# Combination weights turned in one product, output bias as high and low rows: two small TensorE steps of a two-layer hybrid block

## The chip, the cores and the metric

The kernel runs on one core of a Trainium2 chip. The metric is the time of one launch on the device in microseconds (us), the median of several runs. The core has TensorE (PE, matrix products; its weight loads are listed as PEld), VectorE (DVE), ScalarE (ACT), GpSimd (POOL), and SyncE (SP), which here only issues DMAs. Products land in eight banks of PSUM, `bank[0]` to `bank[7]`; PE, DVE and ACT can reach them, POOL works in SBUF.

## The reference

Four rows of 1024 tokens with 128 features in fp32 pass four residual steps. Cut to what matters here:

```python
x = x + attn_a(layernorm(x))     # per-token linear attention over 16 heads, then an MLP
x = x + ffn(layernorm(x))        # 32 experts, top 8
x = x + attn_b(layernorm(x))     # causal window of 64 keys, 16 heads of 8
x = x + ffn(layernorm(x))        # the same experts again

# ffn
probs = softmax(x @ gate_w.T)                 # 32 experts
top_w, top_idx = top_k(probs, 8); top_w /= sum(top_w)
comb = sum(one_hot(top_idx, 32) * top_w)      # a weight per token and expert, most are 0
out = sum_e comb[:, e] * ((x @ up_e.T) * silu(x @ gate_e.T)) @ down_e.T

# the end of attn_b
return ctx @ w_out.T + b_out
```

All 32 experts are computed for all tokens; `comb` weighs their hidden units.

## The kernel before, in words

Work goes in groups of 512 tokens (`GT`), four blocks of 128 (`T = 4`). A row has two groups. There are 16 expert stages (4 rows, 2 groups, 2 ffn steps). A stage is 16 chunks of 128 hidden units (two experts of 64). For a chunk `n`, PE makes the gate and the up product, each as three f32r products of high and low parts (L1522 to L1524); ACT applies silu (L1064); DVE multiplies with the up product (L1303); POOL multiplies with the combination weights `spread_w` (L881, the "hidden units"); and PE adds the down product to bank 6 (`down`, L1545), which in fp32 is two passes. `down` runs three chunks behind (`LAG`), and ACT, DVE and POOL each have a queue of their own, in order.

All other steps (norms, routing, linear attention, projections) are put between the chunks by a table, `PLAN`, that names for each stage or attention part and each slot the steps to run there. Every engine runs its part of a step at that slot. The attention parts (`"attn"`) have slots of their own, three per tile of 128 tokens. The PE steps share bank 7, `side`: a step waits until the reader of the step before has raised `side_taken` (`side_free`), and its reader waits for `side_ready`.

The steps that the change touches:

- `weighT`, 16 times: after `cnorm` (ACT, L1026) has normed `comb`, [128 tokens, 4 blocks, 32 experts], PE turns it (L1460), four transposes into `side[0:32]`; ACT copies that to `combT` (L1033), 32 partitions of 512 tokens, and then frees `side`. SP's `send_weights` (L664) stores `combT` to `comb_dram`, waits for the landing, and issues the loads that spread each expert's weights over 64 partitions (L676, L681). These feed POOL's hidden units of the next stage.
- `proj`, 8 times: the output projection of attn_b. PE first puts the bias into `side` for all four blocks: one row of ones times one row of bias, in fp32 (L1493). Then four fp32 products with `out_w` add to it (L1497). It stands at slot 20 of the first attention part (group 0), in slot 26 of the later ones, and for group 1 at slot 3 of the next row's first expert stage (of the last rows at like places).
- `mask_rest`, once, on POOL (L814 on): the last of the constants.

The chain of `proj` at slot 3 (`(1, "first")`) begins when `pick` on POOL (L895, L897) has finished `mixT`.

Of the kernel before, what the change touches and what calls it, by code (L numbers as in the profile page):

```python
# [19 lines left out]
F32 = mybir.dt.float32  # L20
F32R = mybir.dt.float32r
BF16 = mybir.dt.bfloat16
I32 = mybir.dt.int32
ALU = mybir.AluOpType
ACT = mybir.ActivationFunctionType
AX_X = mybir.AxisListType.X

P = 128
ROWS, SEQ, D = 4, 1024, 128
T = 4  # L30
GT = T * P
# [4 lines left out]
NE, ED = 32, 64  # L36
# [5 lines left out]
QB = 32  # L42
# [13 lines left out]
DEEP = 3  # L56
# [399 lines left out]
def hybrid_block(nc, x, wqkv_a, lam, g1, g2, g3, w1, w2, wqkv_b, wout, bout, wgate, wg, wu, wd, out):  # L456
# [3 lines left out]
    with ExitStack() as ctx:  # L460
        def sb(name, shape, dt=F32):
            return ctx.enter_context(nc.sbuf_tensor(name, shape, dt))

        def sem(name):
            return ctx.enter_context(nc.semaphore(name))
# [2 lines left out]
        qkv_a_w = sb("qkv_a_w", [P, 3 * D])  # L468
        w1_w, w2_w = sb("w1_w", [P, D]), sb("w2_w", [P, D])
        qkv_b_w, out_w = sb("qkv_b_w", [P, 3 * D]), sb("out_w", [P, D])  # L470
        bout_row = sb("bout_row", [1, D])
        router_w = sb("router_w", [P, NE])
        gate_hi, gate_lo = sb("gate_hi", [P, NE * ED], F32R), sb("gate_lo", [P, NE * ED], F32R)
        up_hi, up_lo = sb("up_hi", [P, NE * ED], F32R), sb("up_lo", [P, NE * ED], F32R)
# [4 lines left out]
        lam_diff, lam_coef = sb("lam_diff", [P, 1]), sb("lam_coef", [P, 1])  # L479

        ident, same_query = sb("ident", [P, P]), sb("same_query", [P, HG, QB], BF16)
        ones_row, ones_col, minus_half = sb("ones_row", [1, P]), sb("ones_col", [P, 1]), sb("minus_half", [P, 1])
        head_bits, head_mask = sb("head_bits", [P, HG, HG]), sb("head_mask", [P, HG])
        q_mask = sb("q_mask", [P, HG])
        window = sb("window", [P, 2, NB, KW], BF16)
# [22 lines left out]
        logits, top, neg_top = sb("logits", [P, T, NE]), sb("top", [P, T, TOP]), sb("neg_top", [P, T])  # L508
        expd, replaced = sb("expd", [P, T, NE]), sb("replaced", [P, T, NE])
        top_sum, top_inv = sb("top_sum", [P, T]), sb("top_inv", [P, T])  # L510
        comb, combT = sb("comb", [P, T, NE]), sb("combT", [NE, 2, GT])

        comb_dram = nc.dram_tensor("comb_dram", (DEEP, NE, GT), F32, kind="Internal").ap()
        spread_w = sb("spread_w", [P, 2, EACH, GT])
# [16 lines left out]
        side = bank[SIDE_BANK]  # L531

        x_loaded, x_stored = [[sem(f"x_loaded_{r}_{g}") for g in range(G)] for r in range(2)], (sem("x_stored_0"), sem("x_stored_1"))
        qkv_a_loaded, attn_a_loaded, small_loaded, down_loaded = (
            sem("qkv_a_loaded"), sem("attn_a_loaded"), sem("small_loaded"), sem("down_loaded"))
        gate_loaded, up_loaded = sem("gate_loaded"), sem("up_loaded")
        pool_const, ident_ready, masks_ready = sem("pool_const"), sem("ident_ready"), sem("masks_ready")
        lam_step, qkv_w_ready, bits_ready, head_mask_ready = (
            sem("lam_step"), sem("qkv_w_ready"), sem("bits_ready"), sem("head_mask_ready"))
        hi_ready, router_ready = sem("hi_ready"), sem("router_ready")  # L540
# [3 lines left out]
        side_ready, side_taken = sem("side_ready"), sem("side_taken")  # L544
# [16 lines left out]
        comb_ready, comb_normed, combT_ready, combT_sent = (  # L561
            sem("comb_ready"), sem("comb_normed"), sem("combT_ready"), sem("combT_sent"))
# [15 lines left out]
        qkv_a_loads = [(qkv_a_w[:], wqkv_a), (g1_col[:], g1.rearrange("(p a) -> p a", a=1))]  # L578
        attn_a_loads = [(lam_row[:], lam.partition_broadcast(P)), (g2_row[:], g2.partition_broadcast(P)),
                        (g3_row[:], g3.partition_broadcast(P)), (w1_w[:], w1), (w2_w[:], w2), (router_w[:], wgate)]  # L580
        small_loads = [(qkv_b_w[:], wqkv_b), (out_w[:], wout), (bout_row[:], bout.rearrange("(a n) -> a n", a=1))]

        def wait(engine, semaphore, count):

            if count > 0:
                engine.wait_ge(semaphore, count)
# [7 lines left out]
        def tile(row, i):  # L594
            return row * TILES + i
# [46 lines left out]
        def _(sp):  # L642
# [17 lines left out]
            def send_weights(fg):  # L660
                sp.wait_ge(combT_ready, fg + 1)
                for of_parity, loaded in enumerate(spread_loaded):
                    wait(sp, loaded, 32 * (1 + of_parity) * (fg - 2))
                sp.dma_start(comb_dram[fg % DEEP], combT[:, fg % 2]).then_inc(combT_sent, 16)  # L664
                sp.wait_ge(combT_sent, 16 * (fg + 1))

            def spread_quarter(fg, q):
# [30 lines left out]

            load_rows(1, 0)
            send_weights(0)  # L700
            spread_quarter(0, 0)
            spread_quarter(0, 1)
# [5 lines left out]
            def next_weights(fg):  # L708
                send_weights(fg)
                spread_quarter(fg, 0)  # L710
                spread_quarter(fg, 1)
# [14 lines left out]
            for period, place, row, f in SCHEDULE:  # L726
# [11 lines left out]
                fg = STAGE_AT[row, f]  # L738
# [18 lines left out]
        def _(pool):  # L757
            consts, steps_done = [0], [0]

            def const(ins):  # L760
                consts[0] += 1
                ins.then_inc(pool_const, 1)
                pool.wait_ge(pool_const, consts[0])
# [8 lines left out]
                               pattern=[[-1, P]], channel_multiplier=1).then_inc(ident_ready, 1)  # L772
            const(pool.memset(ones_col[:], 1.0))
            const(pool.memset(minus_half[:], -0.5))
            const(pool.memset(ones_row[:], 1.0))

            def w_lo(row, n):
                if n == 0:
# [8 lines left out]
            def masks(row, n):  # L787
                (mask_identity, mask_first, mask_rest)[n]()
# [13 lines left out]
            def mask_rows(groups):  # L802
                for j in groups:
                    rows = window[QB * j:QB * (j + 1)]
                    const(pool.affine_select(out=rows, in_=rows, compare_op=ALU.is_gt, fill=NEG, base=0,
                                             pattern=[[0, 2], [0, NB], [1, KW]], channel_multiplier=-1))
                    const(pool.affine_select(out=rows, in_=rows, compare_op=ALU.is_ge, fill=NEG, base=WIN,
                                             pattern=[[0, 2], [0, NB], [-1, KW]], channel_multiplier=1))
# [5 lines left out]
            def mask_rest():  # L814
                pool.wait_ge(kv_terms_ready, TILES)
                mask_rows(range(1, HG))
                for b in range(WIN // QB):
                    const(pool.memset(window[:, 0, b, 0:WIN - QB * b], NEG))

                const(pool.memset(vals[0:WIN, 0, 0], 0.0))  # L820
                pool.memset(keysT[:, 0:WIN], 0.0).then_inc(masks_ready, 1)

# [98 lines left out]
        def _(act):  # L921
# [4 lines left out]
            def side_product(row, name, n):  # L926
                act.wait_ge(side_ready, SIDE_AT[row, name, n] + 1)
# [101 lines left out]
            def weighT(row, f):  # L1029
                fg = STAGE_AT[row, f]  # L1030
                side_product(row, "weighT", f)
                wait(act, combT_sent, 16 * (fg - 1))
                act.activation(combT[:, fg % 2], side[0:NE, :], ACT.Copy).then_inc(combT_ready, 1)  # L1033
                act.wait_ge(combT_ready, fg + 1)
                act.sem_inc(side_taken, 1)

# [29 lines left out]
            def here(name, copy):  # L1066
# [5 lines left out]
                     "qscale": qscale, "h_sq1": h_sq1, "h_sq2": h_sq2, "h_gain": h_gain, "attnT": attnT_step,  # L1072
                     "mlp1": mlp1, "z_hi": z_hi_step, "weigh": weigh, "cnorm": cnorm,
                     "weighT": weighT, "seq_turn": here("seq_turn", seq_turn), "keys": here("keys", keys),
                     "queries": here("queries", queries), "values": values, "seq_copy": seq_turn, "keys_copy": keys,
                     "queries_copy": queries, "lam": lam_step_exp, "lead": lambda row, n: silu(row, 0, n)}
# [314 lines left out]
        def _(pe):  # L1391
            def side_free(row, name, n):
                wait(pe, side_taken, SIDE_AT[row, name, n])
# [62 lines left out]
            def weighT(row, f):  # L1456
                pe.wait_ge(comb_normed, STAGE_AT[row, f] + 1)
                side_free(row, "weighT", f)
                for t in range(T):
                    mm = pe.transpose(side[0:NE, P * t:P * (t + 1)], comb[:, t], ident[:])  # L1460
                mm.then_inc(side_ready, 1)

            def y_back(row, f):
                pe.wait_ge(y_copied, STAGE_AT[row, f] + 1)
# [23 lines left out]
                mm.then_inc(side_ready, 1)  # L1488

            def proj(row, g):  # L1490
                side_free(row, "proj", g)
                pe.wait_ge(mix_picked, tile(row, T * g + T))
                pe.matmul(side.rearrange("p (t d) -> p t d", d=D), ones_row[:],  # L1493
                          bout_row[:].unsqueeze(1).broadcast_to([1, T, D]), start=True, stop=False,
                          skip_group_check=True)
                for t in range(T):
                    mm = pe.matmul(side[:, P * t:P * (t + 1)], mixT[:, T * g + t], out_w[:], start=False,  # L1497
                                   stop=(t == T - 1), skip_group_check=True)
                mm.then_inc(side_ready, 1)

            def gate_up(row, f, s):
# [10 lines left out]
                for w_hi, w_lo, banks, freed, ready in ((gate_hi, gate_lo, GATE_BANKS, silu_ready, gate_ready),  # L1512
# [5 lines left out]
                    elif after is not None:  # L1518
# [8 lines left out]
                     "moe_turn": lambda row, n: turn(row, "m", n, "moe_turn"),  # L1527
                     "seq_turn": lambda row, n: turn(row, "s", n, "seq_turn"), "qkv": qkv_step, "qkv_first": qkv_first, "qkv_next": qkv_next, "attnT": attnT_step,
                     "mlp1": mlp1, "mlp2": mlp2, "route": route, "weighT": weighT, "y_back": y_back, "keys": keys,
                     "queries": queries, "values": values, "proj": proj,  # L1530
                     "early": lambda row, n: gate_up(row, 0, n)}

# [147 lines left out]
```

## Time and profile before

| what | value |
|---|---|
| three runs | 998.98, 1000.45, 1000.55 us (median 1000.45) |
| span of the profiled execution | 997.6 us, from its first to its last instruction |
| around the span | the runs lie 1.4 to 3.0 us above it; the profiled execution's own time is not listed apart |
| busy | PE 91%, POOL 66%, DVE 65%, PEld 63%, ACT 61% |

The profile has a page of sums and a trace of every instruction. Times in rows are us from the span's start unless they say ns. "x4" means four like instructions merged into one row, and the time is then that of all of them. In square brackets stands the idle time of the engine before the instruction and what ended it; "issue" means that nothing the profile shows was waited for. An fp32 product appears as two passes (x2). In rows of the chain a product's time is the part of it that the chain passes through; in the timeline its end is modelled and overlaps the next one.

### The profile page before, as it was taken

The numbers are of one execution on the slowest core, as the hardware profiler recorded it, in microseconds if no ns is written. First come the engines' busy times: TensorE is split into PE (matmuls) and PEld (weight loads), VectorE is DVE, ScalarE is ACT, GpSimd is POOL, SyncE is SP. The second block draws the span as 40 slices with busy tenths as digits, with TensorE's granted clock in tenths as the row PEclk, the third lists the DMA queues.
The fourth block names the chain that finished last, engine by engine and source line by source line (L and its number), as shares of the span: only waits on it lengthen the run. The fifth ranks groups of instructions, "written<-read, shape, count | busy, mean of one in ns | idle before, by whom it ended". The sixth has DMA issues, their size and how long they took to land.

```text
span 997.6 us, 16805 instructions
## 1 busy us (share of the span) xinstructions
PE 911.7 (91%) x5472; PEld 627.0 (63%) x5472; DVE 647.7 (65%) x1447; ACT 611.6 (61%) x1875; POOL 661.2 (66%) x610
## 2 busy tenths in 40 slices
PE   3267899899999999999999999999999998999998
PEld 1144566686666666586666666677666666657665
DVE  5886867688658638697739737787735347437432
ACT  4345566984664575895674575797455377386432
POOL 7676878657688649666759857756765545646554
PEclk8567999989999999999999999999999999999999
DMA  5005252014353524610433534520333560350452
GB/s 185 0 3 135 46 129 72 16 45 108 88 127 87 121 79 96 155 44 12 96 87 88 127 98 85 146 65 18 84 99 81 139 156 12 84 132 12 85 129 63
DMA packets 64762, 85.68 MB, mean 86 GB/s; under 512 B 5218, under 2 KB 30627, under 8 KB 64419
## 3 DMA queue, kind: packets, MB, share of 16 engines
q1 hardware_dynamic: 64674, 84.62, 35.2%
q8 instruction: 43, 0.70, 0.3%
q14 instruction: 45, 0.36, 0.1%
HBM read 79.32 MB, written 5.28 MB: 85 GB/s over the span
## 4 chain that ended last, share of the span: by engine, by line
PE 61%; ACT 11%; POOL 7%; issue 5%; DVE 4%; DVEq 0%; ACTq 0%; POOLq 0%
PE bank L1545 16%; PE bank L1522 8%; PE bank L1524 8%; PE bank L1523 8%; ACT probs L1089 5%; PE bank L1581 4%; PE bank L1566 4%; POOL work L881 3%; PE bank L1595 2%; PE bank L1559 1%; PE bank L1405 1%; POOL kv_terms L846 1%; DVE probsT L1345 1%; PE bank L1399 1%; POOL rstd L833 1%
## 5 line engine op out<-in xcount | busy, mean ns | idle before, releaser
L881 POOL TENSOR_TENSOR work<-work,spread_w 128x512 f32<-128x512 f32 x256 | 336.3, 1325 | 165.4 <-DVE work L1303 162.3
L1303 DVE TENSOR_TENSOR work<-work,bank 128x512 f32<-128x512 f32 x256 | 173.6, 681 | 214.0 <-ACT work L1064 128.1
L1545 PE MATMUL bank<-work,down_w 128*128 128x512 f32 x512 | 263.9, 599 | 9.3 <-POOL work L881 7.4
L1064 ACT ACTIVATE work<-bank 128x512 f32<-128x512 f32 x256 | 151.2, 596 | 182.1 <-PE bank L1524 178.6
L1089 ACT ACTIVATE probs<-bank,neg_max 128x96 f32<-128x96 f32 x512 | 166.0, 382 | 8.2 <-DVE neg_max L1331 5.7
L1522 PE MATMUL bank<-z_hi,gate_hi 128*128 128x512 f32 x256 | 167.0, 652 | 3.6 <-ACT elu L974 2.0
L889 POOL TENSOR_TENSOR probs<-probs,prob_inv 128x768 f32<-128x768 f32 x64 | 94.1, 1470 | 74.0 <-DVE prob_inv L1339 74.0
L1089 ACT ACTIVATION_READ_ACCUMULATOR probs<-bank,neg_max 128x1 f32 x512 | 125.6, 248 | 0.0
L1545 PEld LDWEIGHTS bank<-work,down_w 128*128 128x128 f32 x512 | 94.6, 189 | 40.5 <-POOL work L881 15.0
L1524 PE MATMUL bank<-z_hi,gate_lo 128*128 128x512 f32 x256 | 102.4, 400 | 0.0
L1522 PE MATMUL bank<-z_hi,up_hi 128*128 128x512 f32 x256 | 102.0, 398 | 0.0
L1523 PE MATMUL bank<-z_lo,gate_hi 128*128 128x512 f32 x256 | 101.6, 397 | 0.0
L1524 PE MATMUL bank<-z_hi,up_lo 128*128 128x512 f32 x256 | 101.5, 397 | 0.0
L1523 PE MATMUL bank<-z_lo,up_hi 128*128 128x512 f32 x256 | 100.5, 393 | 0.0
L846 POOL TENSOR_TENSOR kv_terms<-elu,qkv 128x1024 f32<-128x1024 f32 x32 | 84.7, 2649 | 12.7 <-DVE elu L1161 9.8
L1345 DVE COPY probsT<-bank 96x512 f32<-96x512 f32 x128 | 80.4, 667 | 7.1 <-PE bank L1581 6.5
L1331 DVE TENSOR_REDUCE neg_max<-bank 128x4 f32<-128x384 f32 x128 | 64.9, 547 | 23.4 <-PE bank L1566 22.4
L1581 PE MATMUL bank<-ident,probs 128*96 128x128 f32 x512 | 70.9, 281 | 8.2 <-DVE probsT L1345 7.0
L1522 PEld LDWEIGHTS bank<-z_hi,gate_hi 128*128 128x128 f32 x256 | 49.1, 192 | 40.0 <-issue 28.0
L1566 PE MATMUL bank<-keysT,qm 32*128 32x96 f32 x1024 | 70.0, 272 | 0.0
L1523 PEld LDWEIGHTS bank<-z_lo,gate_hi 128*128 128x128 f32 x256 | 49.5, 193 | 32.7 <-issue 29.8
L1566 PEld LDWEIGHTS bank<-keysT,qm 32*128 32x128 f32 x1024 | 67.4, 191 | 0.0
(154 smaller groups left out, 1466.2 us busy)
## 6 DMA issues: line engine op xcount, KB each, us to landing
spread_w<-comb_dram SPq DMA_DIRECT2D x96, 512.0 KB, 6.7
spread_w<-comb_dram SPq DMA_DIRECT2D x128, 128.0 KB, 3.0
vals<-v_dram SPq DMA_DIRECT2D x16, 384.0 KB, 4.1
x_buf<-x SPq DMA_DIRECT2D x8, 256.0 KB, 3.4
v_dram<-v_tok SPq DMA_DIRECT2D x8, 256.0 KB, 4.5
out<-xs SPq DMA_DIRECT2D x8, 256.0 KB, 3.8
spread_w<-wg SPq DMA_DIRECT2D x1, 1024.0 KB, 6.5
spread_w<-wu SPq DMA_DIRECT2D x1, 1024.0 KB, 8.5
```

Of the source, the lines that this page charges most:

```text
L846: pool.tensor_tensor(kv_terms[:, i % 2].rearrange("p (e d h) -> p e d h", e=HD, d=HD), k.unsqueeze(2).broadcast_to([P, HD, HD, H]), v.unsq ...
L881: pool.tensor_tensor(work[:, n % WORK], work[:, n % WORK], spread_w[:, n // EACH % 2, s % EACH], ALU.mult).then_inc(hid_gated, 1)
L889: pool.tensor_tensor(pr, pr, prob_inv[:, i % 2, part].unsqueeze(2).broadcast_to([P, HALF_BLOCKS, KW]), ALU.mult).then_inc(probs_normed, 1)
L1064: act.activation(work[:, n % WORK], bank[GATE_BANKS[ring_of(row, f, s)]], ACT.Silu).then_inc(silu_ready, 1)
L1089: a = act.activation(probs[:, i % 2, m], bank[hg][:, b * KW:(b + 1) * KW], ACT.Exp, bias=neg_max[:, i % 2, m:m + 1], accum_out=prob_sum[:, ...
L1303: dve.tensor_tensor(work[:, n % WORK], work[:, n % WORK], bank[UP_BANKS[ring_of(row, f, s)]], ALU.mult).then_inc(gated_ready, 1)
L1522: pe.matmul(dst, w_hi[:, cols], h, start=True, stop=False)
L1523: pe.matmul(dst, w_hi[:, cols], l, start=False, stop=False)
L1524: pe.matmul(dst, w_lo[:, cols], h, start=False, stop=True).then_inc(ready, 1)
L1545: pe.matmul(bank[Y_BANK], down_w[:, c], work[:, n % WORK], start=(c == 0), stop=(c == CH - 1)).then_inc(down_done, 1)
L1566: mm = pe.matmul(bank[hg][:, KW * b:KW * (b + 1)], qm[feats, i // T, NB * (i % T) + b].rearrange("p j q -> p (j q)"), keysT[feats, first:f ...
L1581: mm = pe.transpose(bank[4 + b % 2][0:KW, P * hg:P * (hg + 1)], probs[:, i % 2, hg * NB + b], ident[:])
```

## The change

The four transposes of a turn become one: `comb` is read as [128 tokens, 128 (block, expert)], and its transpose has (block, expert) in partitions. `combT` becomes 128 partitions of 128 tokens, and the store to `comb_dram` puts each partition's 512 bytes at its block's place; the layout there, and all that reads it, is as before. The bias becomes a matrix of 128 rows that is zero but for row 0, the bias rounded to f32r, and row 32 (`QB`), what the rounding left over; a 128x128 matrix of ones times it, in f32r, gives the bias for all four blocks in one product of one pass. POOL makes both matrices in `mask_rest`, and SP loads the bias a second time, into row 32.

```diff
-        bout_row = sb("bout_row", [1, D])
+        bout_rows = sb("bout_rows", [QB + 1, D])
+        bias_hi, bias_parts = sb("bias_hi", [QB + 1, D], F32R), sb("bias_parts", [P, D], F32R)
...
-        comb, combT = sb("comb", [P, T, NE]), sb("combT", [NE, 2, GT])
+        comb, combT = sb("comb", [P, T, NE]), sb("combT", [T * NE, 2, P])
...
+        small_loads = [(qkv_b_w[:], wqkv_b), (out_w[:], wout), (bout_rows[0:1], bout.rearrange("(a n) -> a n", a=1)),
+                       (bout_rows[QB:QB + 1], bout.rearrange("(a n) -> a n", a=1))]
...
-                sp.dma_start(comb_dram[fg % DEEP], combT[:, fg % 2]).then_inc(combT_sent, 16)
+                sp.dma_start(comb_dram[fg % DEEP].rearrange("e (t p) -> t e p", p=P),
+                             combT[:, fg % 2]).then_inc(combT_sent, 16)
...
-            const(pool.memset(ones_row[:], 1.0))
...
+                const(pool.memset(ones[:].bitcast(F32), 1.0))
+                const(pool.memset(bias_parts[:].bitcast(F32), 0.0))
+                pool.wait_ge(small_loaded, 16 * len(small_loads))
+                low = slice(QB, QB + 1)
+                const(pool.tensor_copy(bias_parts[0:1], bout_rows[0:1]))
+                const(pool.tensor_copy(bias_hi[low], bout_rows[low]))
+                pool.tensor_tensor(bias_parts[low], bout_rows[low], bias_hi[low], ALU.subtract).then_inc(bias_ready, 1)
+                pool.wait_ge(bias_ready, 1)
...
-                act.activation(combT[:, fg % 2], side[0:NE, :], ACT.Copy).then_inc(combT_ready, 1)
+                act.activation(combT[:, fg % 2], side[:, 0:P], ACT.Copy).then_inc(combT_ready, 1)
...
-                for t in range(T):
-                    mm = pe.transpose(side[0:NE, P * t:P * (t + 1)], comb[:, t], ident[:])
-                mm.then_inc(side_ready, 1)
+                pe.transpose(side[:, 0:P], comb[:].rearrange("p t e -> p (t e)"), ident[:]).then_inc(side_ready, 1)
...
+                if row == 0 and g == 0:
+                    pe.wait_ge(bias_ready, 1)
...
-                pe.matmul(side.rearrange("p (t d) -> p t d", d=D), ones_row[:],
-                          bout_row[:].unsqueeze(1).broadcast_to([1, T, D]), start=True, stop=False,
+                pe.matmul(side.rearrange("p (t d) -> p t d", d=D), ones[:],
+                          bias_parts[:].unsqueeze(1).broadcast_to([P, T, D]), start=True, stop=False,
```

On PE, around the turn of the weights in an expert stage (the fourth of the program), these rows stand before. L1545 is the down product, L1522 to L1524 the gate and up products of the next chunk.

```order
L1524 MATMUL bank<-z_hi,up_lo 128x512
L1545 MATMUL bank<-work,down_w 128x512 [waits hid_gated]
L1460 MATMUL bank<-ident,comb 32x128 [waits side_taken,comb_normed]
L1460 MATMUL bank<-ident,comb 32x128 x3
L1522 MATMUL bank<-z_hi,gate_hi 128x512 [waits silu_ready]
```

In the changed kernel, whose lines are numbered 10 or 11 higher there:

```order
L1535 MATMUL bank<-z_hi,up_lo 128x512
L1556 MATMUL bank<-work,down_w 128x512 [waits hid_gated]
L1470 MATMUL bank<-ident,comb 128x128 [waits side_taken,comb_normed]
L1533 MATMUL bank<-z_hi,gate_hi 128x512 [waits silu_ready]
L1534 MATMUL bank<-z_lo,gate_hi 128x512
```

Four transposes have become one, in the same place with the same waits.

On POOL the constants of `mask_rest` stand ahead of the linear attention's products (`kv_terms`) and the first hidden units (L881). Before:

```order
L818 MEMSET window 128x64 [waits pool_const]
L818 MEMSET window 128x32 [waits pool_const]
L820 MEMSET vals 64x128 [waits pool_const]
L821 MEMSET keysT 128x64 [waits pool_const]
L846 TENSOR_TENSOR kv_terms<-elu,qkv 128x1024 [waits kv_summed,elu_ready]
```

And in the changed kernel:

```order
L821 MEMSET window 128x32 [waits pool_const]
L823 MEMSET ones 128x128 [waits pool_const]
L824 MEMSET bias_parts 128x128 [waits pool_const]
L827 CAST bias_parts<-bout_rows 1x128 [waits small_loaded,pool_const]
L828 CAST bias_hi<-bout_rows 1x128 [waits pool_const]
L829 TENSOR_TENSOR bias_parts<-bout_rows,bias_hi 1x128 [waits pool_const]
L831 MEMSET vals 64x128 [waits bias_ready]
L832 MEMSET keysT 128x64 [waits pool_const]
L857 TENSOR_TENSOR kv_terms<-elu,qkv 128x1024 [waits kv_summed,elu_ready]
```

Five instructions are new there, and one of them waits for the small loads as well.

## Rows read from the trace of the kernel before

**Rows 1.** The page, chain of work that ended last, share of the span by engine.
```profile
PE 61%; ACT 11%; POOL 7%; issue 5%; DVE 4%; DVEq 0%; ACTq 0%; POOLq 0%
```
**Rows 2.** The chain in order of time, 312 to 320 us: start us, us, what.
```profile
314.10 0.86 PE bank L1545 x2
314.96 0.44 PE bank L1460 x4
...
315.62 0.23 PE bank L1523
```
**Rows 3.** The chain, 540 to 562 us (L1399: four transposes of 128x128).
```profile
551.43 1.12 PE bank L1545 x2
552.56 0.44 PE bank L1399 x4
```
**Rows 4.** Groups by line and shape: busy us, mean ns of one, idle before.
```profile
L1399 PEld LDWEIGHTS bank<-ident,z 128*128 128x128 f32 x128 | 16.2, 150 | 36.7 <-issue 20.5 <-ACT z L940 16.1
...
L897 POOL TENSOR_TENSOR mixT<-mix_all 128x128 f32<-128x128 f32 x32 | 14.6, 456 | 2.5
...
L952 ACT ACTIVATE elu<-bank 128x256 f32<-128x256 f32 x24 | 9.0, 376 | 0.0
```
**Rows 5.** The chain, 314 to 330 us.
```profile
323.51 1.00 PE bank L1545 x2
```
**Rows 6.** The chain, 360 to 368 us.
```profile
363.06 0.60 ACT combT L1033
```
**Rows 7.** DMA issues (KB, us to landing); timelines of POOL and of PE.
```profile
v_dram<-v_tok SPq DMA_DIRECT2D x8, 256.0 KB, 4.5
...
comb_dram<-combT SPq DMA_DIRECT2D x16, 64.0 KB, 1.6
...
130.47 1.34 POOL L881 TENSOR_TENSOR work<-work,spread_w 128x512 f32<-128x512 f32 x1 [2.17 <-DMA spread_w<-comb_dram]
...
136.88 0.59 PE L1545 MATMUL bank<-work,down_w 128*128 128x512 f32 x1
```
**Rows 8.** The chain, 470 to 476 us.
```profile
473.42 1.05 PE bank L1493 x2
474.47 1.09 PE bank L1497 x8
```
**Rows 9.** The chain, 409 to 412 us (L1486: four fp32 products of 128x128).
```profile
410.24 0.89 PE bank L1486 x8
```
**Rows 10.** Timeline of weight loads (PEld) at 242.7, 243.7 and 946.5 us.
```profile
242.72 0.29 PEld L1493 LDWEIGHTS bank<-bout_row,ones_row 1*128 1x128 f32 x2 [0.76 <-issue]
...
243.77 0.52 PEld L1497 LDWEIGHTS bank<-out_w,mixT 128*128 128x128 f32 x4 [0.76 <-issue]
...
946.76 0.19 PEld L1524 LDWEIGHTS bank<-z_hi,gate_lo 128*128 128x128 f32 x1
```
**Rows 11.** Timeline of POOL and of PE, 474 to 477 us.
```profile
474.29 2.54 POOL L881 TENSOR_TENSOR work<-work,spread_w 128x512 f32<-128x512 f32 x2
...
476.79 0.59 PE L1545 MATMUL bank<-work,down_w 128*128 128x512 f32 x1
```
**Rows 12.** Timeline of POOL and of PE, 244 to 247 us.
```profile
244.49 1.30 POOL L881 TENSOR_TENSOR work<-work,spread_w 128x512 f32<-128x512 f32 x1
...
246.15 0.59 PE L1545 MATMUL bank<-work,down_w 128*128 128x512 f32 x1
```
**Rows 13.** Timeline of DVE and of PE, 230 to 233 us.
```profile
230.33 1.23 DVE L1345 COPY probsT<-bank 96x512 f32<-96x512 f32 x2
...
231.73 1.08 PE L1595 MATMUL bank<-probsT,vals 96*32 96x128 f32 x32
```
**Rows 14.** Timeline of POOL, 69 to 80 us, and of SP at 15 us.
```profile
79.06 2.38 POOL L846 TENSOR_TENSOR kv_terms<-elu,qkv 128x1024 f32<-128x1024 f32 x1 [7.47 <-DVE elu L1161]
...
15.12 0.34 SPq L658 DMA_DIRECT2D bout_row<-bout  x1
```
**Rows 15.** Busy us by engine (PE, PEld, DVE, ACT, POOL), granted clock, DMA; 202.7 to 209.5.
```profile
202.70:209.50 6.80, 6.80 (x65) 5.76 (x63) 3.97 (x20) 5.36 (x33) 3.96 (x4) 0.50 0.01 2
```

More of the change, by code:

```diff
@@ L481, in hybrid_block @@
         ident, same_query = sb("ident", [P, P]), sb("same_query", [P, HG, QB], BF16)
-        ones_row, ones_col, minus_half = sb("ones_row", [1, P]), sb("ones_col", [P, 1]), sb("minus_half", [P, 1])
+        ones, ones_col, minus_half = sb("ones", [P, P], F32R), sb("ones_col", [P, 1]), sb("minus_half", [P, 1])
         head_bits, head_mask = sb("head_bits", [P, HG, HG]), sb("head_mask", [P, HG])
@@ L537, in hybrid_block @@
         pool_const, ident_ready, masks_ready = sem("pool_const"), sem("ident_ready"), sem("masks_ready")
+        bias_ready = sem("bias_ready")
         lam_step, qkv_w_ready, bits_ready, head_mask_ready = (
@@ L580, in hybrid_block @@
                         (g3_row[:], g3.partition_broadcast(P)), (w1_w[:], w1), (w2_w[:], w2), (router_w[:], wgate)]
-        small_loads = [(qkv_b_w[:], wqkv_b), (out_w[:], wout), (bout_row[:], bout.rearrange("(a n) -> a n", a=1))]
+        small_loads = [(qkv_b_w[:], wqkv_b), (out_w[:], wout), (bout_rows[0:1], bout.rearrange("(a n) -> a n", a=1)),
+                       (bout_rows[QB:QB + 1], bout.rearrange("(a n) -> a n", a=1))]
         def wait(engine, semaphore, count):
```

## The prediction

> **What bounds the kernel now.** I read the chain of work that ended last first: 61% of the span runs through TensorE (PE), and the next engine, ScalarE (ACT), has 11% [rows 1]. Then I went down the chain stretch by stretch, in order of time, and looked for the lines that the change touches. From 112 us on, where the chain begins, it holds all 8 bias products (L1493, two passes each) and 14 of the 16 turns of the combination weights (L1460, four transposes each); the turns at 70 us, ahead of its beginning, and at 544 us are not on it. In the expert stages a chunk is six f32r products of 0.23 us and one fp32 product of two passes at 0.86 us, with no gap between them [rows 2]. So what PE is spared there is time, unless another engine stands close behind. I therefore also compared, after each edit, when POOL finished a chunk's hidden units with when PE's down product (L1545) took them.
>
> **The turn of the weights.** Before: four transposes with 32 columns of weights, 0.44 us on the chain [rows 2]. After: one with 128. Four transposes with 128 columns of weights each also take 0.44 us [rows 3], so the width of the stationary side does not show and one should take 0.11. Bounds: 0.11 if it goes on at that pace, 0.15 if its weight load (150 ns in [rows 4]) stands bare. I take 0.15, the cautious end, since a single one has no neighbour to hide behind: 0.29 spared per turn; the upper bound is 0.33.
>
> Where it counts: at 70 us PE is not on the chain (it goes on to wait for other engines): nothing. At 315 us the down product two chunks on already waited for POOL (1.00 instead of 0.86 us at 323.51, [rows 5]): nothing. At 544 us the chain runs through POOL and comes back to PE only with the down product at 551.43, which waited for POOL too [rows 3]: nothing. At 228 us see below. The other twelve give 12 x 0.29 = 3.5 us.
>
> ACT's copy of the result shrinks from 32x512 to 128x128. The copy takes 0.60 us at 363.06 [rows 6]; a copy of 256 columns takes 0.376 [rows 4], so 128 columns lie under that, and by the slope between those two (0.22 us over 256 columns) at 0.27. Spared: 0.22 to 0.33 us, I take 0.3, and it counts once only, at 363 us, where PE waits for this copy to free the side bank [rows 6]. Together the turn is worth 3.8 us.
>
> **The store of the weights.** It becomes 128 runs of 512 B instead of 32 of 2 KB, the same 64 KB. Bounds: the 1.6 us of now, and the 4.5 us of a store of 512 such runs [rows 7]. Behind it on SP's queue stand its own wait for the landing and then the eight loads that spread the weights; POOL waits for those. Only one such wait is in the trace, 2.17 us before 130.47, and the down product of that chunk comes at 136.88, 5.1 us after POOL is done [rows 7]. A store later by 2.9 us (4.5 - 1.6), less 0.6 us by which turn and copy are earlier, stays inside that: price 0. If the cover were gone it would cost up to 2.3 us at one stage.
>
> **The bias product.** Before: two fp32 passes of 512 columns with one row of weights, 1.05 us, and then four fp32 products with `out_w` (eight passes), 1.09 us [rows 8]. The nearest rows without a one-row neighbour are eight passes of the same shape at 0.89 us [rows 9], and an f32r pass of 512 columns over 128 rows at 0.23 [rows 2]. Why 1.09 and not 0.89? The weight loads tell: the load before the first one-row pass and the load before `out_w` each come only after 0.76 us of idle time, at the moment the product itself starts; between products that use all 128 rows the next load runs while the product before it is still going, with no idle time [rows 10]. With 128 rows of ones that change of rows is gone. Spared: 1.05 + 1.09 - 0.23 - 0.89 = 1.02 us each; if the 0.2 us of the loads stays, 0.82; if the load behind f32r stays too and the one-row pass is to be taken at the 0.43 us of a normal fp32 pass, 2 x 0.43 - 0.23 = 0.63. I take 1.02, since the new shape is that of the f32r rows.
>
> The Trainium skill, "TensorE: Matmul & The Clock Gate", Part 3 "The mechanism", says under what overlaps and what doesn't that a weight load overlaps a running matmul only when its row group differs. By that rule the widening would take an overlap away, and each bias product would pay its weight load bare, 0.19 us more by the load in [rows 10], 1.5 us over eight. The loads of [rows 10] show the contrary: those with the same rows overlap, those with other rows wait; the sum goes by the rows.
>
> Where it counts. At 465, 694, 853 and 920 us nothing stands close; at 473 us, and likewise at 702, POOL's next hidden units end at 475.56 (half of the pair from 474.29) and PE takes them at 476.79, so 1.2 us are free [rows 11]: six times 1.02 = 6.1 us. At 242 us POOL's next hidden units end at 245.79 and PE takes them at 246.15 [rows 12]: only 0.3 us is to be had, and then PE waits for POOL. At 223 us, with the turn at 228 us, PE would win 1.3 us, but the next mix needs VectorE's two copies, which run from 230.33 to 231.56 behind ACT's exponentials, and PE now begins that mix at 231.73 [rows 13]. Two of its four blocks can go before, so I take 0.85 for both edits together. Sum 7.2 us.
>
> **What is added at the start.** POOL gets two fills of 128x128, two casts and one subtraction of one row, less one fill of before, each with a wait for itself; the largest near row is a 128x128 product at 456 ns [rows 4], so at most 5 x 0.46 + 5 x 0.1 = 2.8 us, and hardly under 1. They stand right before the work that POOL begins at 79.06 after 7.47 us idle [rows 14], so they cost nothing; bare they would cost those 1 to 2.8 us once. The wait for the small loads is behind them in time too: SP issued them by 15 us [rows 14]. One more DMA like the 0.34 us of that row delays SP's next load, at a time when its rows are not yet wanted. PE's wait for the bias is over by the first product at 223 us.
>
> **Sum.** 3.8 + 7.2 = 11.0 us. The profiled span is 997.6 us, so 986.6. The median of the runs, 1000.45, lies 2.85 us above that span; I add the same: 989.4 us.
>
> **Rivals.**
> A, the sum above, 0.55, own range 986 to 992.5 (986: turns at 0.11, and what was cut off at 223, 242 and 315 us won as well; 992.5: 0.82 per bias product and two more places lost to POOL).
> B, other engines close up, 0.20: PE is spared all this, but POOL or ACT take over in more places than the three I found. For: the down product already waited for POOL at 323.51 and 551.43 [rows 3, 5], and what PE gains in one place brings it nearer to POOL in the next. Against: gaps of 1.2 us and more at the six main places. Half of 11.0 left: 994.9.
> C, the row change is not what costs, 0.10: the bias product gives 0.63 each. Six times 0.63, 0.3 and 0.6 are 4.7, with the turns 3.8: 8.5, so 992.0. The same page, "Why this matters for your kernels", says of small K that one matmul with 32 rows takes the time of one with 128; by that, rows as such bring nothing, and only the passes count. The 1.05 us of [rows 8] beside 0.86 of [rows 2] speaks against it.
> D, more than the sum, 0.06: PE runs at half clock from 202.7 to 209.5 us (granted 0.50, its lower level of 1.2 GHz, [rows 15]), so up to half of those 6.8 us is lost to the clock. Shifted work could miss such a stretch: 3.4 us, 986.0.
> E, no change within 0.2% (2 us, about what the runs' spread lets one tell), 0.05: POOL and ACT take nearly all, 999.5.
> F, slower, 0.04: the same clock, the other way. PE is busy less, and in the attention parts, where it waits for probabilities, the granted clock may fall more often. Each stretch like that of [rows 15] costs 3.4 us, so from four new ones the gain is gone; five give 989.4 + 17 = 1006. Against: what is spared is about 1% of PE's work, spread over 24 places.
>
> **The numbers.** Predicted 989.4, the time of A. The range from 985.5 to 996.0 holds A, B, C and most of D; E, F and some of B, about 0.15, lie outside. Faster by over 0.2%: A to D, 0.91; within: 0.05; slower: 0.04.
>
> **What would show it.** Right: the bias product as one f32r pass of about 0.23 us on the chain, the `out_w` products behind it at 0.9, no 0.76 us of idle time before their loads; the turn at 0.11 to 0.15; ACT's copy near 0.27; POOL's idle time at the start shorter by 1 to 3 us with the same end. Wrong: longer idle times of PE before the down product, put down to POOL; a turn that takes over 0.2 us; POOL waits for the spread weights that weren't there; more stretches at half clock.

## The result, and the profile after

The changed kernel took 983.0 us (median of four runs, 981.75 to 991.83), the kernel before 999.72 (the three runs on record and a fourth at 994.83); the ratio is 0.9854 [0.9808, 0.99]. That is 16.7 us less where 11.0 were forecast, and 983.0 lies below the stated range; but 11.0 us less would be a ratio of 0.989, which the interval does not exclude. The profiled execution has a span of 980.9 us, at a mean granted clock of 0.966 (before: 997.6 at 0.962). Two later comparisons of the same two kernels gave 0.9898 [0.9862, 0.9934] and 0.989 [0.9846, 0.9934]. So the size of the gain itself has to be explained. (All ratios here leave out runs more than 1.5% slower than the fastest of their kernel, two of `after_again` and one of `turn_only`; medians, ranges and the line drawn through the runs below keep them.)

The page after: the busy line, and the chain by engine, which answers to [rows 1].

```profile
PE 894.5 (91%) x5416; PEld 618.2 (63%) x5416; DVE 648.3 (66%) x1447; ACT 604.8 (62%) x1875; POOL 663.2 (68%) x614
...
PE 56%; ACT 12%; POOL 8%; DVE 6%; issue 5%; DVEq 0%; ACTq 0%; POOLq 0%
```

PE's share of the chain falls from 61% to 56%, VectorE's (DVE) rises from 4% to 6%. The steps themselves on the chain (start us, us, what), at three places: a turn in an expert stage (answers to [rows 2]), the turn with ACT's copy that was at 363 us (to [rows 6]), and a bias product with its `out_w` products (to [rows 8]). L1470 is the turn, L1044 the copy, L1504 the bias product, L1508 `out_w`, L1556 the down product.

```profile
263.05 0.86 PE bank L1556 x2
263.91 0.11 PE bank L1470
264.02 0.23 PE bank L1533
...
353.49 0.12 PE bank L1470
...
353.64 0.28 ACT combT L1044
...
455.69 0.23 PE bank L1504
455.93 0.89 PE bank L1508 x8
```

0.11 instead of 0.44, 0.28 instead of 0.60, 0.23 instead of 1.05, and 0.89 instead of 1.09: every changed step has, to 0.01 us, the length that the prediction's more hopeful bound gave it. The weight loads beside them (timeline of PEld; idle time before in brackets) answer to [rows 10]:

```profile
235.27 0.19 PEld L1504 LDWEIGHTS bank<-bias_parts,ones 128*128 128x128 f32 x1 [0.24 <-issue]
235.70 1.10 PEld L1508 LDWEIGHTS bank<-out_w,mixT 128*128 128x128 f32 x8 [0.24 <-issue]
...
455.42 0.19 PEld L1504 LDWEIGHTS bank<-bias_parts,ones 128*128 128x128 f32 x1
455.53 1.09 PEld L1508 LDWEIGHTS bank<-out_w,mixT 128*128 128x128 f32 x8
```

The 0.76 us of idle time are gone. At 455.42 the load runs ahead of its product's part of the chain (455.69), behind the transposes that are still going. POOL's constants (timeline; answers to [rows 14]), and the one wait for spread weights (to [rows 7]):

```profile
71.26 0.20 POOL L823 MEMSET ones<- 128x128 f32 x1
71.52 0.21 POOL L824 MEMSET bias_parts<- 128x128 f32 x1
71.80 1.34 POOL L827 CAST bias_parts<-bout_rows 1x128 fp32r<-1x128 f32 x1
73.20 0.28 POOL L828 CAST bias_hi<-bout_rows 1x128 fp32r<-1x128 f32 x1
73.57 0.45 POOL L829 TENSOR_TENSOR bias_parts<-bout_rows,bias_hi 1x128 fp32r<-1x128 f32 x1
...
79.14 2.40 POOL L857 TENSOR_TENSOR kv_terms<-elu,qkv 128x1024 f32<-128x1024 f32 x1 [4.65 <-DVE elu L1172]
...
129.33 1.28 POOL L892 TENSOR_TENSOR work<-work,spread_w 128x512 f32<-128x512 f32 x1 [2.99 <-DMA spread_w<-comb_dram]
```

POOL's idle time before 79.14 shrinks from 7.47 to 4.65 us, and the linear attention's products begin 0.08 us later than before: hidden. The new instructions and their waits take 2.8 us together, which is the prediction's upper bound, though one of them takes 1.34 us and not at most 0.46. SP (timeline) issues the first spreading load 2.47 us after the store; in the kernel before it was 1.65 us:

```profile
123.14 0.56 SPq L667 DMA_DIRECT2D comb_dram<-combT  x1
125.61 4.96 SPq L680 DMA_DIRECT2D spread_w<-comb_dram  x8
```

POOL's wait grows from 2.17 to 2.99 us, and the down product of that chunk comes no later against its neighbours. The cover held.

**Where the 16.7 us came from.** Both kernels run the same 256 down products in the same order. The start of each in the one trace less its start in the other is what has been gained up to there; the steps in that difference show where. (Inside the attention parts, where no down product runs, the other PE instructions that both kernels share serve for it.) This list is called the ledger below. Summed by cause, for the two profiled executions:

| cause | places and steps (us) | sum |
|---|---|---|
| turn | eleven places of 0.28 to 0.33 (chunks 12, 43, 91, 107, ...), and 0.66 at the copy at 363 us | 4.2 |
| bias | 1.04, 1.02, 1.06, 1.01, 1.00 and 0.84 at the six free places; 0.22 at 242; 0.66 at 223 | 6.9 |
| given back | in the routing at 489 us | -0.5 |
| clock, start | ahead of the first down product | 1.65 |
| clock | 3.41 and 1.07 around 189 to 209 us, 1.43 at 346, -1.00 and -0.42 at 819 to 826, small ones | 4.5 |

The first three rows are the change: 10.6 us. At 315 and 544 us the turn gave 0.33 us each, and 0.30 and 0.33 of it were lost at the down product that waits for POOL. What was given back at 489 us went to DVE: in the kernel before, the routing's products (L1450) follow the down product there without a gap; in the changed kernel they (L1461) wait for DVE's `z_lo`, as its chain shows:

```profile
474.52 0.69 DVE z_lo L1269
475.22 0.04 issue
475.26 0.30 PE bank L1461
```

The last two rows are told by the granted clock (PEclk, the number before the last two; 0.50 is the lower level, 1.2 GHz, 1.00 the upper, 2.4 GHz). Windows, us, busy of PE, PEld, DVE, ACT, POOL, clock, DMA; first the kernel before at its start:

```profile
76.40:83.20 6.80, 5.25 (x13) 3.73 (x12) 4.85 (x11) 4.05 (x7) 3.62 (x2) 0.50 0.66 192
```

Then the changed kernel:

```profile
78.60:84.00 5.40, 5.20 (x20) 3.54 (x20) 4.58 (x11) 2.64 (x5) 3.65 (x2) 1.00 0.81 209
...
92.50:819.00 726.50, 696.11 (x4367) 486.21 (x4366) 502.65 (x1144) 484.05 (x1523) 505.13 (x454) 1.00 0.38 91
...
816.00:830.00 14.00, 12.77 (x133) 10.16 (x130) 10.50 (x28) 11.07 (x53) 9.98 (x13) 0.76 0.00 1
```

At the start the kernel before stays at half clock up to 83.2 us, the changed one only up to 78.6: from 80.5 us on its f32r products follow each other every 0.23 us where the same ones took 0.43, and that is the 1.65 us. The half clock that the kernel before has at 202.7 [rows 15] is not there at the corresponding work, nor are two shorter stretches (189 and 346 us), as the changed kernel has the upper level from 92.5 to 819 us; one of 6.8 us at 819 is new. Two theories: **sum** (theory 1 in the expectations), the change is worth its 10.6 us and the clock falls differently in every execution; **clock** (theory 2), the changed work keeps the clock up and that is part of its gain.

### The profile page after: what moved, and what is told of

Read it like the earlier page. It is cut to its first block, busy times and chain, and to the rows that moved or that the text cites. A ratio compares the mean times of both kernels' runs of the same rounds, so it can differ in the third digit from the quotient of the medians.

```text
span 980.9 us, 16699 instructions
## 1 busy us (share of the span) xinstructions
PE 894.5 (91%) x5416; PEld 618.2 (63%) x5416; DVE 648.3 (66%) x1447; ACT 604.8 (62%) x1875; POOL 663.2 (68%) x614
## 4 chain that ended last, share of the span: by engine, by line
PE 56%; ACT 12%; POOL 8%; DVE 6%; issue 5%; DVEq 0%; ACTq 0%; POOLq 0%
PE bank L1556 15%; PE bank L1533 8%; PE bank L1535 8%; PE bank L1534 8%; ACT probs L1100 5%; PE bank L1592 4%; PE bank L1577 3%; POOL work L892 3%; PE bank L1606 2%; POOL kv_terms L857 1%; DVE probsT L1356 1%; PE bank L1570 1%; POOL rstd L844 1%; PE bank L1416 1%; DVE work L1314 1%
## 5 line engine op out<-in xcount | busy, mean ns | idle before, releaser
L1556 PE MATMUL bank<-work,down_w 128*128 128x512 f32 x512 | 263.5, 598 | 10.3 <-POOL work L892 8.5
L1556 PEld LDWEIGHTS bank<-work,down_w 128*128 128x128 f32 x512 | 94.0, 188 | 42.1 <-POOL work L892 16.8
L1592 PEld LDWEIGHTS bank<-ident,probs 128*96 128x96 f32 x512 | 54.3, 128 | 20.2 <-issue 12.2
```

Source lines behind the costliest of these rows:

```text
L1556: pe.matmul(bank[Y_BANK], down_w[:, c], work[:, n % WORK], start=(c == 0), stop=(c == CH - 1)).then_inc(down_done, 1)
L1592: mm = pe.transpose(bank[4 + b % 2][0:KW, P * hg:P * (hg + 1)], probs[:, i % 2, hg * NB + b], ident[:])
```

## The experiments

**Both kernels once more, and each half of the change alone.** `before_again` and `after_again` have nothing edited.

> The kernel before, unchanged. Theory 1 (the change itself is worth about 10.6 us, and the rest of the 16.7 us between the two first profiles is where TensorE's clock happened to fall): the runs of this kernel differ among themselves by some 5 us, those with a higher mean granted clock are the shorter ones, and in the profile the stretches at half clock lie elsewhere than at 189, 203 and 346 us, or are fewer; the fastest run comes to about 994. Theory 2 (the change itself keeps the clock up): all runs lie within 2 us of 1000, with the same stretches at half clock in the profile.

> The changed kernel, unchanged. Theory 1: runs from 982 to 992, the longer ones at a lower mean clock; the profile shows half clock at other places than 819 us; the median is 10 to 14 us under that of the kernel before in the same rounds. Theory 2: 16 to 18 us under it, and hardly a stretch at half clock after 100 us.

`turn_only` is the kernel before with the turn's edits (`combT`, its store and its copy too; here the part on PE):

```diff
...
-                for t in range(T):
-                    mm = pe.transpose(side[0:NE, P * t:P * (t + 1)], comb[:, t], ident[:])
-                mm.then_inc(side_ready, 1)
+                pe.transpose(side[:, 0:P], comb[:].rearrange("p t e -> p (t e)"), ident[:]).then_inc(side_ready, 1)
```

> Only the turn of the combination weights is changed; the bias product is as before. The ledger of the two profiles gives 0.32 us for each of 12 turns and 0.66 us for the one at 363 us, together 4.2 us where both profiles run at full clock; predicted were 3.8. So landmark by landmark 4 us, and the median 3 to 5 us under the kernel before, if the clock falls alike. Theory 2 would have it either near 4 or near 10, as the clock goes with the turn or not.

`bias_only` is the changed kernel with the turn undone; its small buffers lie in space that is not yet in use:

```diff
-                pe.transpose(side[:, 0:P], comb[:].rearrange("p t e -> p (t e)"), ident[:]).then_inc(side_ready, 1)
+                for t in range(T):
+                    mm = pe.transpose(side[0:NE, P * t:P * (t + 1)], comb[:, t], ident[:])
+                mm.then_inc(side_ready, 1)
...
+        bout_rows, bias_hi = mix_all[0:QB + 1, 0:D], yT[0:QB + 1, 0:D].bitcast(F32R)
...
```

> Only the bias product is changed; turn, copy and store of the weights are as before. (The loaded bias rows and the rounded row lie in space that other tiles use later, since the wider copy of the weights leaves too little.) Predicted: 1.02 us at six places, 0.3 at 242 us and 0.85 with the turn at 228 us; together about 7 us, and the median 5.5 to 8.5 us under the kernel before if the clock falls alike; 11 or more if it is the bias product that keeps the clock up (theory 2).

Measured on one chip, the kernel before at 1000.85 us (35 runs, 993.15 to 1006.57):

| kernel | median, range (12 runs each) | ratio to the kernel before |
|---|---|---|
| before_again | 1003.47, 999.19 to 1007.70 | 1.0042 [1.0015, 1.007] |
| turn_only | 995.22, 989.11 to 1003.98 | 0.9957 [0.9923, 0.999] |
| bias_only | 992.23, 988.14 to 997.97 | 0.9928 [0.9897, 0.9959] |
| after_again | 990.34, 982.74 to 999.87 | 0.9898 [0.9862, 0.9934] |

The turn alone brings 4.3 us, the bias 7.2, both 10.2: near the sum of 11.0 and far from 16.7. Unedited code is 0.4% off itself here, by more than its own interval, so a single median says no more than some 4 us either way. Two expected ranges were missed: the fastest run of `before_again` was to be about 994 and is 999.19, and the runs of `after_again` were to end at 992 and go up to 999.87. The ledger is sharper: the turn's steps are 0.29 to 0.33 us in `turn_only`, the bias steps 0.85 to 1.05 at the six free places in `bias_only`, each at the places of the table above.

And the clock moves without any edit. Windows of `before_again`:

```profile
180.00:196.00 16.00, 13.62 (x122) 9.98 (x120) 10.48 (x29) 12.15 (x64) 10.92 (x11) 0.79 0.01 3
652.00:666.00 14.00, 14.00 (x115) 11.89 (x114) 8.83 (x18) 8.96 (x56) 6.22 (x6) 0.51 0.01 2
```

The same program has half clock from 652 to 666 us where [rows 15]'s execution has none, and full clock at 202.7, where that one has half. Between these two traces of identical code the ledger runs from 3.1 us ahead to 3.8 us behind; the stretch at 652 costs 5.9 us by itself, and the first down product begins at 83.75 in place of 84.90. So shifts as large as the two clock rows of the table come without any edit.

**The changed kernel a third time**, on another chip.

> The changed kernel once more, nothing edited, timed anew beside the kernel before. Theory 'sum' (the change itself is worth 10.6 us, the rest of the first 16.7 us was where the clock happened to fall): 10 to 12 us under the kernel before, and at the same mean granted clock, run against run, 10.5 to 12 us. Rival 'more' (the first comparison was right and the second one unlucky): 15 us or more, also at the same clock.

989.18 us (six runs, 984.85 to 996.05) against 1000.99 (11 runs): 11.8 us, ratio 0.989 [0.9846, 0.9934]. In its profile the changed kernel has the half clock near 189 and 203 us again that was missing in the first:

```profile
183.20:190.00 6.80, 6.80 (x66) 5.67 (x66) 3.52 (x8) 5.98 (x28) 4.71 (x7) 0.50 0.00 1
200.20:210.50 10.30, 10.30 (x83) 8.80 (x84) 6.05 (x24) 7.44 (x41) 4.08 (x4) 0.50 0.08 21
```

To compare at the same clock I put a straight line of time over mean granted clock through the 104 runs that list both (kernel before 58, changed 22 with the first four, `turn_only` and `bias_only` 12 each): one slope, one level for each kernel. A clock higher by 0.01 goes with 7.0 us less, and runs scatter by 1.4 us around the line. At 0.960 the levels are 1001.0 before, 989.8 changed, 996.7 turn, 994.8 bias: **-11.2 (+-0.7)**, -4.3 (+-0.9) and -6.2 (+-0.9) us, with 95% intervals. The 22 runs of the changed kernel have a median of 990.0 and a mean clock of 0.9601, the 58 of the kernel before 1001.1 and 0.9598. So the theory "clock" falls: over many runs the mean clock of the two kernels agrees to 0.0003 (95%: within 0.003, 2 us by the line), and of the 6.1 us of the two clock rows nothing is left between the levels. The first four runs had a mean of 0.9655; without them the changed kernel's mean is 0.9589.

**What the one row of weights cost.** Two kernels take the widening and the number format apart. `bias_f32_rows128` keeps the 128 rows and goes back to fp32:

```diff
-        bias_hi, bias_parts = sb("bias_hi", [QB + 1, D], F32R), sb("bias_parts", [P, D], F32R)
+        bias_parts = sb("bias_parts", [P, D])
...
-        ones, ones_col, minus_half = sb("ones", [P, P], F32R), sb("ones_col", [P, 1]), sb("minus_half", [P, 1])
+        ones, ones_col, minus_half = sb("ones", [P, P]), sb("ones_col", [P, 1]), sb("minus_half", [P, 1])
...
```

> The bias product of the changed kernel, but in fp32 (two passes) with the bias itself in row 0: all 128 rows of ones and of the bias matrix stay, the high and low parts go. It computes the same result. Theory 'rows' (the 0.2 us that the old bias product lost twice came from its one row of weights): two passes take 0.86 us on the chain, the out_w products behind them stay at 0.89, and the weight loads of both show no 0.76 us of idle time; against the changed kernel each of the six free places loses 0.63 us. Rival 'passes' (rows don't matter, only the number format does): the bias product takes 1.05 us and the out_w products 1.09 again, with 0.76 us of idle time before the loads, and each place loses 1.02 us.

`bias_f32r_rows33` keeps f32r and gives up the widening:

```diff
-                pe.matmul(side.rearrange("p (t d) -> p t d", d=D), ones[:],
-                          bias_parts[:].unsqueeze(1).broadcast_to([P, T, D]), start=True, stop=False,
+                pe.matmul(side.rearrange("p (t d) -> p t d", d=D), ones[0:QB + 1],
+                          bias_parts[0:QB + 1].unsqueeze(1).broadcast_to([QB + 1, T, D]), start=True, stop=False,
```

> The changed kernel with its bias product in f32r as it is, but over the first 33 rows of the two matrices only. It computes the same result. Theory 'rows': the change of rows is back on both sides of the bias product, so its load and the load of out_w come late again with some idle time before them (0.1 to 0.76 us), the product takes 0.4 to 0.45 us instead of 0.23 and the out_w products 1.09 instead of 0.89; each free place loses about 0.4 us. Rival 'passes': 0.23 and 0.89 us as in the changed kernel, loads early, nothing lost.

The chain of `bias_f32_rows128` (L1500 the bias product, L1504 `out_w`), and its weight loads:

```profile
470.80 0.86 PE bank L1500 x2
471.66 0.89 PE bank L1504 x8
```

```profile
470.21 0.19 PEld L1500 LDWEIGHTS bank<-bias_parts,ones 128*128 128x128 f32 x1 [0.24 <-issue]
470.64 0.19 PEld L1500 LDWEIGHTS bank<-bias_parts,ones 128*128 128x128 f32 x1 [0.24 <-issue]
471.07 0.19 PEld L1504 LDWEIGHTS bank<-out_w,mixT 128*128 128x128 f32 x1 [0.24 <-issue]
```

The chain of `bias_f32r_rows33` at the same place, and its loads:

```profile
466.19 0.42 PE bank L1504
466.61 1.09 PE bank L1508 x8
```

```profile
466.12 0.18 PEld L1504 LDWEIGHTS bank<-bias_parts,ones 33*128 33x128 f32 x1 [0.76 <-issue]
466.54 0.97 PEld L1508 LDWEIGHTS bank<-out_w,mixT 128*128 128x128 f32 x8 [0.24 <-issue]
```

Over 128 rows, fp32 takes two passes of 0.43 us and nothing extra: 0.86, and 0.89 behind it. Over 33 rows, f32r takes 0.42 instead of 0.23, and `out_w` 1.09 instead of 0.89: 0.2 us on each side of the change of rows. The loads tell why: with 128 rows they start 0.6 us ahead of their product's part of the chain (470.21 against 470.80), with 33 rows 0.07 us ahead, after 0.76 us of idle time (466.12 against 466.19), and `out_w`'s load at 466.54 again only 0.07 us ahead. In the ledger against the changed kernel the six free places lose 0.61 to 0.67 us with fp32, as forecast from 0.86 - 0.23, and with 33 rows five of them lose 0.38 to 0.40, forecast 0.4. At the sixth (920 us before) it is 0.19: PE waits there for `mixT`, which hides one of the two changes of rows. Both kernels get 0.35 us back at 489 us, where the changed kernel's PE waits for DVE. Theory "rows" holds, "passes" falls: of the 1.02 us at a place, 0.4 come from the widening and 0.63 from the format. (A single run each: 993.84 us at a clock of 0.956, 987.76 at 0.966; by themselves these times tell nothing of so small a cost.)

The Trainium skill, "TensorE: Matmul & The Clock Gate", Part 3 "The mechanism", says under what overlaps and what doesn't that a weight load overlaps a running product only where its row group differs. These two kernels show the contrary once more: loads of the same 128 rows run 0.6 us ahead, and the change to 33 rows leaves 0.07 us.

**What held the gain at 242 us.** In `rstd_later` a step of 2.5 us on POOL moves one slot back:

```diff
-        0: back(("m_stats", 2), ("m_rstd", 2)) + own(("kvsum", 6)),
-        1: own(("wterm", 6)),
+        0: back(("m_stats", 2)) + own(("kvsum", 6)),
+        1: own(("wterm", 6)) + back(("m_rstd", 2)),
```

> The changed kernel with one step of the table moved: the reciprocal deviations (m_rstd, 2.5 us on POOL, 1.94 us of it one power) of group 1's norm in the first expert stage of the second row go from slot 0 to slot 1. Theory (POOL holds what the bias product gave at 242 us): PE no longer waits 0.53 us for POOL's hidden units before the second down product behind the bias product, the part of the bias product's 1.02 us that was missing there (0.7 us) comes out, and it is kept to the end of that stage. Rival (the mix or another engine holds PE there as well): 0.2 us or less, or it is lost again within three chunks.

PE's next down product behind the bias product, in the changed kernel (timeline of PE):

```profile
238.91 1.13 PE L1556 MATMUL bank<-work,down_w 128*128 128x512 f32 x2 [0.53 <-POOL work L892]
```

and in `rstd_later`:

```profile
242.70 0.59 PE L1556 MATMUL bank<-work,down_w 128*128 128x512 f32 x1
```

(The execution had lost 4.5 us before that place, with half clock at 187 and 201 us.) The wait is gone and the ledger gains 0.7 us there, as forecast. Of these, 0.13 are lost two chunks on, 0.06 at the turn of the same stage and 0.12 as the next one begins, so 0.4 us stay; that it would all be kept to the end of the stage was wrong. POOL was what held the gain at 242 us. With 985.21 us in a single run it is not shown to be faster than the changed kernel; 0.4 us is under what the medians can tell.

## Why the prediction was right in its sum and wrong in its time

**The sum held.** Predicted 11.0; the ledger of the first two traces gives 10.6, the runs at equal clock 11.2 (+-0.7). By terms: the turn 3.8 predicted and 4.2 in the ledger, since it is 0.11 us and not the cautious 0.15; its weight load hides after all. The copy on ACT was 0.3 and is 0.32. The bias was 7.2 and is 6.9: about 1.02 at each of five free places, 0.84 at 920 us, the one place where PE waits for `mixT` (0.7 us, in both kernels) and part of the old cost was already hidden; 0.3 and 0.22 at 242; 0.85 and 0.66 at 223 with the turn behind it. The row change is what it was said to be, so rival C is out. The costs at nothing (POOL's start, the store, the places at 315 and 544 us) were nothing. POOL took back only what was named; VectorE took back 0.5 us in the routing at 489 us, which was not: rival B explains 5% and not half. (One figure does not follow from its working: the items given for the lower end of rival A add up to 2.0 us, which is 987.4 and not 986.)

**The step that failed is the one from the sum to the time**: "The profiled span is 997.6 us, so 986.6. The median of the runs, 1000.45, lies 2.85 us above that span; I add the same", and with it the range; rival E put "about what the runs' spread lets one tell" at 2 us. That step took the half-clock stretches of one execution for a property of the kernel. In the executions compared, three of them (189, 202.7 and 346 us) were missing after the change and one came, 4.5 us in all; the start, with less half clock, was 1.65 us shorter. Together 6.1 us, less 0.4 by which the change gave less than forecast, are the 5.7 us from 986.6 to the span of 980.9. The other 0.7 us up to 983.0 lie in the 2.85: every run that lists both is 1.68 to 1.80 us longer than its own span, so the rest of the 2.85 was the distance of one execution from the median of three. Rival D named the cause but priced one stretch with 0.06, and tied it to shifted work. `before_again` shows that no edit is needed: the same code differs from itself by up to 3.8 us along the ledger, and 35 runs of the kernel before spread over 13 us. Three runs within 1.6 us of each other hid that. The 22 runs of the changed kernel have a median of 990.0, 0.6 us from the forecast; that the base of three runs (1000.45) lay so near the median of 58 (1001.1) was luck. Of the four that were timed first, three lie at the fast end (981.75 to 983.41).

What stays open: which execution gets which stretches. That they differ between runs of one program is shown; what starts one was not tested, nor whether the first four runs' higher clock (0.9655) was chance or their chip.

## What to carry to other kernels

A product over few rows (here 1 and 33) between products over all 128 is not cheap: widen it with zeros, and price a step by the weight loads on both sides of it, not by its own length. Sum a change place by place, and ask at each who would be late next; then compare two traces by the start of the same instruction, which separates 0.3 us of change from 5 us of clock. Before a range is set, let unchanged code be compared with itself, and compare runs at the same granted clock.

## What the runs showed of the hardware that was not expected

- Behind the first 92 us, identical code has half-clock stretches at other places in other executions, from 3.4 to 13.7 us long, some inside work in which PE is busy all the time (14.00 of 14.00 us in the window at 652). By the ledger the 13.7 us at 652 cost 5.9, the two at 189 and 203 us (10.2 together) 4.5, and the 3.4 at 346 us 1.4.
- A cast of a single row of 128 values took POOL 1.34 us, the next one of the same shape 0.28, while a fill of 128x128 took 0.20. The conversion is not the reason: in `bias_f32_rows128` a plain fp32 copy of that row takes 1.34 too. Why the first one is long was not tested.
- The store with 512-byte pieces holds SP 0.56 to 0.64 us at all 16 places (0.31 to 0.35 with 2 KB pieces), and at 123 us the spreading loads behind it come 0.82 us later (2.47 against 1.65), for the same 64 KB.
